# Copies of every second half issued by ScalarE in a graph attention kernel

## The chip, the cores and the metric

The kernel runs on one core of a Trainium2 chip. The metric is the device time of one execution in microseconds (us), from three runs of the kernel before. One further execution was profiled; the rows below are its.

## The reference

A pre-normed graph attention layer over 12,500 nodes with 128 features and 200,000 edges, sorted by target node, with 64 features each. There are four heads of 32 features.

```python
h = jnp.maximum(_layernorm(x), 0.0)
h = (h @ W_node.T).reshape(num_nodes, H, HD)
e = (edge_features @ W_edge.T).reshape(num_edges, H, HD)
att = jnp.sum(jnp.concatenate([h[src], h[tgt], e], axis=-1) * a, axis=-1)
att = jnp.where(att > 0, att, 0.2 * att)
m = jnp.maximum(segment_max(att, tgt), 0.0)
ex = jnp.exp(att - m[tgt])
denom = segment_sum(ex, tgt) + (num_edges - deg)[:, None] * jnp.exp(-m)
h_prime = segment_sum((ex / denom[tgt])[:, :, None] * h[src], tgt)
x = x + h_prime.reshape(num_nodes, H * HD)
```

## The kernel before

**Front.** The nodes are taken in 14 groups of 7 blocks of 128. VectorE computes mean and variance; VectorE, ScalarE and Pool normalise 2, 1 and 4 of the 7 blocks (`ON_DVE`, `ON_ACT`, lines 257, 314, 377, 518); TensorE transposes and projects them (`project`, line 637); ScalarE copies the result out of PSUM in three pieces (`evacuate`, line 530), and SyncE stores it in a table in DRAM: per node 128 projected features and 4 source scores. `s_thirds` counts the first two pieces, for the last group only. TensorE's next projection waits until all three pieces of the group before are out (`rows`).

**Edges.** Edges lie in 1563 tiles of 128, and a tile that touches two blocks of target nodes takes two slots: 1660 slots are in use, in 52 groups of 32, each of two halves of 16. One group is one turn of the loop, fully unrolled, in which each engine has its own program, called `body` (lines 866 to 1382); engines meet only in semaphores:

- Pool gathers the table rows of one tile at a time with an indirect DMA into a ring of 32 tiles (`gather`, line 156; loop at line 899). Eight at a time, it first waits until the ring's old tiles have been copied out (`copied`).
- SyncE copies slots from the ring into one of three half-group buffers, `halves` (`copies`, line 815). Eight copies make a batch. For each batch it loads four gather counts and eight ring places from SBUF into registers (lines 825 and 829), waits until all earlier copies have landed (line 833) and until the gathers have (line 835), and then issues eight DMAs of 66 KB. Half `h` must wait for `vals` of half `h - 3`, whose buffer it takes (line 817). In turn `g` SyncE loads flags (842), the edge features (846), stores edge scores (850, which waits for ScalarE's `edge_out`), and then issues the copies of halves `2g + 3` and `2g + 4`.
- VectorE (`body`, line 1350) adds up the scores: `zs` at line 1191 waits for all 32 copies of its group. Then come running maxima per target, the argument of the exponential (1266), the weighted rows of each half (`weighted_rows`, 1274, whose end is the semaphore `vals`), a one-hot matrix of targets per half (`make_onehot`, 1162), and the addition of TensorE's sums to the accumulator (`adds`, 1323).
- TensorE (`body`, line 997) forms the sums as one-hot times rows, three slots at a time in six batches a half (`sums`, 960), the target scores (`target_parts`, 950), the edge scores of a later group (937) and the targets per slot (`slot_targets`, 915). The last waits for `edge_out` of the tile group five ahead. In turn `g` three batches of the first half stand behind it.
- ScalarE (`body`, line 1101) takes two exponentials and a rescaling factor (1061, 1065, 1071), starts the load of the keys (1050), copies the edge scores out of PSUM (`edge_scores_out`, 1023, the semaphore `edge_out`), turns the keys into a one-hot matrix in two passes (`compare_keys`, 1053) and casts the targets (`targets_out`, 1029). In the last turn, 51, it also makes the two one-hots (`last_onehot`, 1122), from absolute difference and rectifier, and in turn 50 it issues the last four copies (`last_copies`, 1135).

The order on each engine is the order of the calls in its `body`. A finishing stage normalises and adds `x`.

Of the kernel before, what the change touches and what calls it, by code (L numbers as in the profile page):

```python
# [14 lines left out]
P = 128  # L15
# [4 lines left out]
G = 32  # L20
# [29 lines left out]
def gat_kernel(nc, x, src, tiles, tile_ends, ea, w_node, w_edge, a, out):  # L50
# [12 lines left out]
    with ctx:  # L63
# [97 lines left out]
        with ExitStack() as stage:  # L161
# [95 lines left out]
            ON_DVE, ON_ACT = 2, 1  # L257
# [4 lines left out]
            with nc.Block(no_gpsimd_drain=True) as block_:  # L262
                @block_.sync
                def _(sp):
# [5 lines left out]
                    def store_last(g):  # L270
                        for n, (b0, b1) in enumerate(((0, 3), (3, 6), (6, W))):
                            if n < 2:
                                sp.wait_ge(s_thirds, n + 1)
                            else:
                                sp.wait_ge(n_["rows"], g + 1)
# [33 lines left out]
                def _(pool):  # L309
                    def normalise(g):  # L310
# [3 lines left out]
                        for w in range(ON_DVE + ON_ACT, W):  # L314
# [26 lines left out]
                def _(dve):  # L341
# [31 lines left out]
                    def normalise(g):  # L373
# [3 lines left out]
                        for w in range(ON_DVE if g else W):  # L377
# [129 lines left out]
                def _(act):  # L507
# [6 lines left out]
                    def normalise(g):  # L514
# [3 lines left out]
                        for w in range(ON_DVE, ON_DVE + ON_ACT):  # L518
# [11 lines left out]
                    def evacuate(g):  # L530
# [5 lines left out]
                        first = S.copy(rows[:, q, 0:3, :], v3(h_bank[0], WP))  # L536
                        second = S.copy(rows[:, q, 3:6, :], v3(h_bank[1], WP))
                        S.copy(rows[:, q, 6, :], h_bank[2]).then_inc(n_["rows"], 1)
                        if g + 1 == N_NODE_GROUPS:
                            first.then_inc(s_thirds, 1)  # L540
                            second.then_inc(s_thirds, 1)
# [81 lines left out]
                def _(pe):  # L623
# [13 lines left out]
                    def project(g):  # L637
                        pe.wait_ge(n_["hn_t"], g + 1)
                        if g:
                            pe.wait_ge(n_["rows"], g)  # L640
                        else:
                            pe.wait_ge(s_wp, 1)
                        for n in range(W):
                            last = T.matmul(h_bank[n // 3][:, (n % 3) * WP:(n % 3 + 1) * WP], hn_t[g % 2][:, n * P:(n + 1) * P], w_proj[:, :],
# [109 lines left out]
        with ExitStack() as stage:  # L754
# [57 lines left out]
            with nc.Block() as block:  # L812
                @block.sync
                def _(sp):
# [51 lines left out]
                    def body(g, prev, nxt, second):  # L866
# [9 lines left out]
                        for h in (2 * g.n + 3, 2 * g.n + 4):  # L876
                            if h < 2 * NG:
                                copies(h, range(GS // BATCH if h < 2 * NG - 1 else 1))

# [31 lines left out]
                def _(pe):  # L911
# [48 lines left out]
                    def sums(g, a, batches):  # L960
# [10 lines left out]
                        if 0 in batches:  # L971
                            pe.wait_ge(s["vals"], g.n * 2 + a + 1)
                            pe.wait_ge(s["onehot"], g.n * 2 + a + 1)
# [46 lines left out]
                def _(act):  # L1020
# [37 lines left out]

                    def exponentials(g):
# [62 lines left out]
                    def last_onehot(g, a, count):  # L1122
                        of_slot = sel_f[:, 0, 0:GS + LAST]
# [402 lines left out]
```

## Time and profile before

| what | value |
|---|---|
| median of 3 runs | 2974.41 us (2969.7 to 2981.4) |
| profiled execution, its own time | 3012.78 us |
| its span | 3011.0 us, granted TensorE clock 0.649 |
| busy: PE, VectorE, ScalarE, Pool | 1245.5, 1442.5, 558.8, 1529.1 us |
| gathers by Pool | 1563, mean 949 ns |
| copies from the ring by SyncE | 1656 of 66 KB; four more by ScalarE |

The span reaches from the first to the last instruction. The busy time leaves out the issuing of DMAs, so SyncE, which does nothing else, has no line there; its work is seen in the timeline of its queue (SPq). "Idle before" in a row is the engine's idle time just ahead, with what ended it.

### The profile page before, as it was taken

How to read it: one execution, taken by the hardware profiler on the slowest of the kernel's cores; microseconds unless marked ns; L12 is line 12 of the kernel's file. 1: busy time of each engine (PE TensorE's matmuls, PEld its weight loads, DVE VectorE, ACT ScalarE, POOL GpSimd, SP SyncE). 2: the span in 40 equal slices, each digit the busy share in tenths (PEclk: the TensorE clock that was granted, in tenths of full speed). 3: DMA queues.
4: the chain of work that ended last, by engine and by line, in shares of the span. 5: the costliest groups of instructions: out<-in, count | busy, mean ns of one | idle time of the engine just before them, and what ended most of it. 6: DMA issues, size and time to landing. Idle time of an engine off the chain costs nothing. (4 is left out here: it accounts for less than half of the span.)

```text
span 3011.0 us, 30562 instructions
## 1 busy us (share of the span) xinstructions
PE 1245.5 (41%) x7204; PEld 932.6 (31%) x7205; DVE 1442.5 (48%) x3419; ACT 558.8 (19%) x629; POOL 1529.1 (51%) x1634
## 2 busy tenths in 40 slices
PE   5432534434434434434353343444344434333335
PEld 5222423323322323323232232333233223223333
DVE  8334545345344445445364453544444534544448
ACT  6211212112111211112111121121121211211213
POOL 6654545555554555555455555555455545554540
PEclk9766656666656666667666666666666656655667
DMA  6443434444344434444343344444344443333335
GB/s 228 147 136 100 136 111 122 118 110 123 114 110 117 119 108 129 115 114 135 107 124 119 108 136 111 116 124 115 109 123 109 136 117 96 112 95 95 95 88 165
DMA packets 333239, 360.72 MB, mean 120 GB/s; under 512 B 57725, under 2 KB 289565, under 8 KB 320135
## 3 DMA queue, kind: packets, MB, share of 16 engines
q1 hardware_dynamic: 272231, 191.42, 20.5%
q0 software_dynamic: 50304, 107.57, 15.7%
q10 hardware_dynamic: 10528, 59.78, 6.1%
q8 instruction: 62, 1.02, 0.1%
q14 instruction: 114, 0.93, 0.1%
HBM read 229.63 MB, written 18.57 MB: 82 GB/s over the span
## 5 line engine op out<-in xcount | busy, mean ns | idle before, releaser
L157 POOL DMA_INDIRECT gath<-node_table,src_i x1563 | 1483.5, 949 | 1385.7 <-DMA gath<-gath 875.6
L979 PE MATMUL bank<-vals,onehot 128*128 128x137 f32 x1992 | 438.5, 389 | 231.0 <-issue 159.6
L979 PEld LDWEIGHTS bank<-vals,onehot 128*128 128x128 f32 x1992 | 412.3, 290 | 259.1 <-issue 192.7
L979 PE MATMUL ps_oht<-vals,onehot 128*128 128x137 f32 x1328 | 304.2, 393 | 191.1 <-issue 160.8
L1334 DVE TENSOR_TENSOR acc<-acc,bank 128x411 f32 x374 | 198.0, 529 | 381.5 <-remote 232.7
L1191 DVE TENSOR_TENSOR zs<-gath,te 128x128 f32<-128x128 f32 x52 | 19.7, 379 | 741.4 <-DMA gath<-gath 561.2
L979 PEld LDWEIGHTS ps_oht<-vals,onehot 128*128 128x128 f32 x1328 | 281.6, 293 | 210.5 <-issue 182.7
L970 PE MATMUL bank<-block_1h,zero_b 128*128 128x411 bf16 x311 | 117.7, 430 | 491.5 <-issue 263.1
L1061 ACT ACTIVATE bank<-arg 128x128 f32<-128x128 f32 x52 | 14.6, 281 | 1515.8 <-DVE arg L1266 1410.5
L1334 DVE TENSOR_TENSOR acc<-acc,ps_oht 128x411 f32 (+1 forms) x248 | 131.6, 531 | 262.2 <-remote 167.1
L956 PE MATMUL bank<-tgt_slot,onehot_t 128*128 128x12 bf16 x1664 | 84.9, 182 | 373.8 <-issue 361.7
L1278 DVE TENSOR_TENSOR vals<-gath,bank 128x2048 f32<-128x2048 f32 x104 | 236.8, 2277 | 0.0
L1166 DVE TENSOR_TENSOR onehot<-bank,rel_s 128x2048 f32<-128x2048 f32 x102 | 232.6, 2281 | 0.0
L970 PE MATMUL ps_oht<-block_1h,zero_b 128*128 128x411 bf16 x208 | 81.1, 429 | 338.7 <-issue 186.3
L1055 ACT ACTIVATE onehot_t<-onehot_t,pcol 128x4096 bf16<-128x4096 bf16 x50 | 185.3, 3707 | 97.7 <-DMA onehot_t<-key_rows 75.5
L970 PEld LDWEIGHTS bank<-block_1h,zero_b 128*128 128x128 bf16 x311 | 28.8, 105 | 556.0 <-issue 299.8
L956 PEld LDWEIGHTS bank<-tgt_slot,onehot_t 128*128 128x128 bf16 x1664 | 68.9, 100 | 383.8 <-issue 369.3
L1057 ACT ACTIVATE onehot_t<-onehot_t,iota 128x4096 bf16<-128x4096 bf16 x50 | 185.4, 3708 | 1.6
L937 PE MATMUL bank<-eattr,w_eatt 128*32 128x512 f32 x360 | 181.8, 651 | 1.7 <-issue 1.7
L970 PEld LDWEIGHTS ps_oht<-block_1h,zero_b 128*128 128x128 bf16 x208 | 19.7, 104 | 384.8 <-issue 212.3
L1031 ACT CAST tgt_slot<-bank 128x384 bf16<-128x384 f32 x52 | 24.7, 476 | 389.5 <-remote 384.2
L1027 ACT COPY edge_out<-bank 32x512 f32<-32x512 f32 x49 | 28.2, 575 | 282.6 <-PE bank L937 183.6
(240 smaller groups left out, 1256.8 us busy)
## 6 DMA issues: line engine op xcount, KB each, us to landing
gath<-gath SPq DMA_DIRECT2D x1656, 66.0 KB
onehot_t<-key_rows ACTq DMA_DIRECT2D x52, 1024.0 KB
eattr<-edge_attr_in SPq DMA_DIRECT2D x43, 1024.0 KB
gath<-node_table,src_i POOLq DMA_INDIRECT x1563
node_table<-onehot SPq DMA_DIRECT2D x13, 462.0 KB, 3.5
acc<-x_in SPq DMA_DIRECT2D x10, 448.0 KB, 5.5
edge_s<-edge_scores SPq DMA_DIRECT2D x11, 256.0 KB
edge_scores<-edge_out SPq DMA_DIRECT2D x43, 64.0 KB
```

The source lines that it names most:

```text
L157: nc.gpsimd.indirect_dma_start(out=ring[:, t % RING, :], out_offset=None, in_=table, in_offset=bass.IndirectOffsetOnAxis(ap=src_i[:, t:t + ...
L937: last = T.matmul(ps_edge, w_eatt[:, c, :], eattr_of(t)[:, c, :], start=(c == 0), stop=(c == 3))
L956: last = T.matmul(ps_te[:, 3 * HEADS * slot:3 * HEADS * (slot + 1)], onehot_t[:, slot, :], tgt_slot[:, :, slot], start=True, stop=True)
L970: T.matmul(SUM_BANK[n % DEPTH][:, 0:SPAN * ACC], zero_b[:, :], block_1h[:, 0:SPAN * ACC], start=True, stop=False)
L979: last = T.matmul(at, onehot[:, a, j, :], vals[:, a, j, :], start=not wide, stop=j == BATCHES[b][-1])
L1027: S.copy(edge_out[:, t % 2, :], ps_edge).then_inc(s["edge_out"], 1)
L1031: S.copy(tgt_slot[:, :, :].rearrange("p c s -> p (c s)"), ps_tgt_slot).then_inc(s["tgt_slot"], 1)
L1055: S.activation(onehot_t[:, :, :], onehot_t[:, :, :], ACT.Abs, bias=pcol[:, 0:1], scale=-1.0).then_inc(s["apart"], 1)
L1057: S.activation(onehot_t[:, :, :], onehot_t[:, :, :], ACT.Relu, bias=iota[:, 1:2], scale=-1.0).then_inc(s["oht"], 1)
L1166: V.tensor_tensor(onehot[:, a, :, :], ps_iota.unsqueeze(1).broadcast_to((P, GS, P)), rel_s[:, ds(g.n * G + a * GS, GS)].unsqueeze(2).broad ...
L1278: V.tensor_tensor(vh[:, :, :, 0:HD], halves[:, (2 * g.n + a) % 3, 0:count, 0:NODE_DIM].rearrange("p s (h c) -> p s h c", h=HEADS), ex.unsq ...
L1334: V.tensor_tensor(a_blk, a_blk, SUM_BANK[(done_batches(g, a, b) - 1) % DEPTH][:, 0:wide * ACC], ALU.add).then_inc(s["added"], 1)
```

## The change

In the front, `ON_DVE` becomes a list: 2 for groups 0 to 11, then 3 and 4, so Pool does 3 and 2 blocks in the last two groups. Every group's first two pieces are counted by `s_thirds`, and `project` waits for the piece of PSUM that it overwrites rather than for all three.

In the loop, ScalarE issues the copies of half `2g + 3` in turns 0 to 49, after the load of keys and ahead of `edge_scores_out`, `compare_keys` and `targets_out`. The new function is like SyncE's. It waits for `vals` first and loads its registers then. SyncE keeps half `2g + 4`, and the eight copies of the last half that it had. The conditions between copies are the same: each batch still waits until all earlier ones have landed.

In turn 50 too ScalarE makes the two one-hots in place of VectorE; they and those of turn 51 count in `last_apart` alone, and TensorE waits for that.

```diff
-            ON_DVE, ON_ACT = 2, 1
+            ON_DVE, ON_ACT = [2] * (N_NODE_GROUPS - 2) + [3, 4], 1
...
                     def project(g):
                         pe.wait_ge(n_["hn_t"], g + 1)
-                        if g:
-                            pe.wait_ge(n_["rows"], g)
-                        else:
+                        if not g:
                             pe.wait_ge(s_wp, 1)
                         for n in range(W):
+                            if g and n == 6:
+                                pe.wait_ge(n_["rows"], g)
+                            elif g and n % 3 == 0:
+                                pe.wait_ge(s_thirds, 2 * g - 1 + n // 3)
...
                             store_edges(t)
-                        for h in (2 * g.n + 3, 2 * g.n + 4):
-                            if h < 2 * NG:
-                                copies(h, range(GS // BATCH if h < 2 * NG - 1 else 1))
-
+                        if second:
+                            copies(2 * g.n + 4)
+                        if g.n + 2 == NG:
+                            copies(2 * NG - 1, range(1))
...
                             pe.wait_ge(s["vals"], g.n * 2 + a + 1)
-                            pe.wait_ge(s["onehot"], g.n * 2 + a + 1)
+                            if g.n + 2 < NG:
+                                pe.wait_ge(s["onehot"], g.n * 2 + a + 1)
+                            else:
+                                pe.wait_ge(s["last_apart"], 2 * (2 * (g.n + 2 - NG) + a + 1))
...
+                    def copies(h):
+                        act.wait_ge(s["vals"], h - 2)
+                        for b in range(GS // BATCH):
+                            n = h * (GS // BATCH) + b
+                            if n == 3 * (GS // BATCH):
+                                act.wait_ge(s_landed, 4)
+                            _, ready = nc.values_load_multi_w_load_instructions(
+                                ready_row[:, n * READY:(n + 1) * READY], engines=[mybir.EngineType.Activation], min_val=16 * BLK, max_val=16 * BLK * -(-NB_TILES // READY))
+                            _, places = nc.values_load_multi_w_load_instructions(
+                                place_row[:, n * BATCH:(n + 1) * BATCH], engines=[mybir.EngineType.Activation], min_val=0, max_val=RING - 1,
+                                skip_runtime_bounds_check_because="the front masks the places with the ring's length less one")
+                            act.wait_ge(s["copied"], 16 * BATCH * n)
+                            for q, landed in enumerate(ready):
+                                act.wait_ge(s_g[q], landed)
+                            for j, place in enumerate(places):
+                                act.dma_start(halves[:, h % 3, b * BATCH + j, :], ring[:, ds(place, 1), :].rearrange("p o r -> p (o r)")).then_inc(s["copied"], 16)
...
-                        if not nxt:
+                        if not second:
                             last_onehot(g, 0, GS)
                         exponentials(g)
                         rescale_factor(g)
-                        if not nxt:
-                            last_onehot(g, 1, LAST)
                         if g.n + 2 == NG:
                             last_copies(g + 1)
+                        if not second:
+                            last_onehot(g, 1, GS if nxt else LAST)
                         if (g.n + 2) % CG == 0 and (g.n + 2) // CG < NCH:
                             cast_sel((g.n + 2) // CG)
                         if second:
                             load_keys(g + 2)
+                            copies(2 * g.n + 3)
                         if g.n + AHEAD < NTG:
                             edge_scores_out(g.n + AHEAD)
...
                         weighted_rows(g, 0)
-                        if nxt:
+                        if second:
                             make_onehot(g, 0)
...
                         weighted_rows(g, 1, GS if nxt else LAST)
+                        if second:
+                            make_onehot(g, 1)
                         if nxt:
-                            make_onehot(g, 1)
                             key_flags(g + 1)
```

Two places show how instructions move. The first is ScalarE's program in one turn, from its load of the keys to its next exponential. Before:

```order
L1050 DMA onehot_t<-key_rows 128x4096 [waits scores_ps]
L1027 COPY edge_out<-bank 32x512 [waits edge_scores_stored0,edge_ps]
L1055 ACTIVATE onehot_t<-onehot_t,pcol 128x4096 [waits key_rows_loaded]
L1057 ACTIVATE onehot_t<-onehot_t,iota 128x4096 [waits apart]
L1031 CAST tgt_slot<-bank 128x384 [waits tgt_slot_ps]
L1061 ACTIVATE bank<-arg 128x128 [waits arg]
```

Of the change the same turn, the end of the second batch of copies first, up to the start of the next turn's copies:

```order
L1076 DMA gath<-gath 128x132
L1029 COPY edge_out<-bank 32x512 [waits edge_scores_stored0,edge_ps]
L1057 ACTIVATE onehot_t<-onehot_t,pcol 128x4096 [waits key_rows_loaded]
L1059 ACTIVATE onehot_t<-onehot_t,iota 128x4096 [waits apart]
L1033 CAST tgt_slot<-bank 128x384 [waits tgt_slot_ps]
L1080 ACTIVATE bank<-arg 128x128 [waits arg]
L1084 ACTIVATE enm<-m 128x128 [waits vals,m]
L1090 ACTIVATE alpha<-cols,first_ind 128x4 [waits scaled,cols]
L1052 DMA onehot_t<-key_rows 128x4096 [waits scores_ps]
L1067 TENSOR_LOAD rows_i [waits vals]
L1067 ISA x8
L1069 TENSOR_LOAD rows_i
```

Between the load of the keys and the copy of edge scores there now stand two batches, each two register loads with eight instructions on registers and eight copies, behind waits for `vals`, gathers and landings. ScalarE's program grows from 619 rows to 2525.

The second place is SyncE's program, from the last copy of a half on (`ISA` is an instruction on registers). Before, ahead of the second of the two halves of a turn:

```order
L837 DMA gath<-gath 128x132
L825 TENSOR_LOAD rows_i [waits vals]
L825 ISA x8
L829 TENSOR_LOAD rows_i
L837 ISA [waits tiles_gathered2,tiles_gathered1,tiles_gathered3,tiles_gathered0,copied]
```

Of the change:

```order
L836 DMA gath<-gath 128x132
L841 DMA flag_row<-chunk_flags 4x2x128 [waits cfirst]
L845 DMA eattr<-edge_attr_in 128x2048 [waits edge_ps]
L849 DMA edge_scores<-edge_out 32x4x128 [waits edge_out]
L824 TENSOR_LOAD rows_i [waits vals]
L824 ISA x8
L828 TENSOR_LOAD rows_i
L836 ISA [waits tiles_gathered2,tiles_gathered1,tiles_gathered3,tiles_gathered0,copied]
```

After one half SyncE goes straight to the next turn's loads and to the store that waits for `edge_out`. TensorE's order in the loop is unchanged.

## Rows read from the trace of the kernel before

**Rows 1.** The page: busy time of each engine.

```profile
PE 1245.5 (41%) x7204; PEld 932.6 (31%) x7205; DVE 1442.5 (48%) x3419; ACT 558.8 (19%) x629; POOL 1529.1 (51%) x1634
```

**Rows 2.** Waits: who waited for whom, us in total, times, longest.

```profile
DVE zs L1191 <- DMA gath<-gath: 561.2, 37, 28.4
...
SPq L835 <- DMA gath<-node_table,src_i: 32.9, 42, 1.4
```

**Rows 3.** Source line 1191: durations in ns, first and last start in us.

```profile
L1191 DVE TENSOR_TENSOR zs<-gath,te x52: 376/379/382, 166.8 to 2952.1; 128x128 f32<-128x128 f32 x52
```

**Rows 4.** Timeline of SyncE, 1669 to 1722 us: start, us, what, count.

```profile
1669.77 13.69 SPq L837 DMA_DIRECT2D gath<-gath  x8
...
1669.77 23.39 SPq L837 DMA_DIRECT2D gath<-gath  x16
...
1695.98 0.73 SPq L850 DMA_DIRECT2D edge_scores<-edge_out  x1
1708.75 12.36 SPq L837 DMA_DIRECT2D gath<-gath  x16
```

**Rows 5.** Timeline of VectorE in the same group.

```profile
1665.62 0.38 DVE L1191 TENSOR_TENSOR zs<-gath,te 128x128 f32<-128x128 f32 x1 [13.29 <-DMA gath<-gath]
...
1666.92 1.73 DVE L1334 TENSOR_TENSOR acc<-acc,bank 128x411 f32 x3
...
1688.35 0.26 DVE L1282 TENSOR_TENSOR vals<-enm,last_s 128x64 f32<-128x64 f32 x1
...
1723.17 0.38 DVE L1191 TENSOR_TENSOR zs<-gath,te 128x128 f32<-128x128 f32 x1 [13.11 <-issue]
```

**Rows 6.** Timeline of SyncE at 1538 us, eight copies.

```profile
1538.21 5.04 SPq L837 DMA_DIRECT2D gath<-gath  x8
```

**Rows 7.** Timeline of Pool: its gathers, 1661 to 1706 us.

```profile
1661.11 0.94 POOL L157 DMA_INDIRECT gath<-node_table,src_i  x1 [1.89 <-issue]
...
1678.81 0.94 POOL L157 DMA_INDIRECT gath<-node_table,src_i  x1 [0.30 <-issue]
...
1704.94 0.94 POOL L157 DMA_INDIRECT gath<-node_table,src_i  x1 [0.30 <-issue]
```

**Rows 8.** Timeline of PE, matmuls, 1671 to 1709 us.

```profile
1671.97 0.84 PE L956 MATMUL bank<-tgt_slot,onehot_t 128*128 128x12 bf16 x24
...
1683.73 2.87 PE L979 MATMUL bank<-vals,onehot 128*128 128x137 f32 x12
...
1698.99 1.74 PE L979 MATMUL bank<-vals,onehot 128*128 128x137 f32 x6 [5.04 <-issue]
...
1708.08 0.39 PE L979 MATMUL ps_oht<-vals,onehot 128*128 128x137 f32 x1 [1.71 <-issue]
```

**Rows 9.** Timeline of ScalarE, 1683 to 1698 us.

```profile
1683.96 0.28 ACT L1061 ACTIVATE bank<-arg 128x128 f32<-128x128 f32 x1 [27.32 <-DVE arg L1266]
1684.17 0.29 ACT L1065 ACTIVATE enm<-m 128x128 f32<-128x128 f32 x1
...
1690.42 0.57 ACT L1027 COPY edge_out<-bank 32x512 f32<-32x512 f32 x1 [5.76 <-issue]
...
1694.63 3.71 ACT L1057 ACTIVATE onehot_t<-onehot_t,iota 128x4096 bf16<-128x4096 bf16 x1
```

**Rows 10.** Timeline of ScalarE's queue: its four copies near the end.

```profile
2942.46 2.95 ACTq L1148 DMA_DIRECT2D gath<-gath  x4
```

**Rows 11.** Timelines of Pool and ScalarE at 2831 us.

```profile
2830.84 0.94 POOL L157 DMA_INDIRECT gath<-node_table,src_i  x1 [0.30 <-issue]
...
2831.53 0.28 ACT L1061 ACTIVATE bank<-arg 128x128 f32<-128x128 f32 x1 [33.42 <-DVE arg L1266]
2832.93 0.31 ACT L1065 ACTIVATE enm<-m 128x128 f32<-128x128 f32 x1 [1.12 <-remote]
```

**Rows 12.** The one-hots: VectorE's group, and ScalarE's sixteen pieces in turn 51.

```profile
L1166 DVE TENSOR_TENSOR onehot<-bank,rel_s 128x2048 f32<-128x2048 f32 x102 | 232.6, 2281 | 0.0
...
2953.90 4.78 ACT L1130 ACTIVATE onehot<-iota,sel_f 128x128 f32<-128x128 f32 x16 [8.24 <-PE bank L979]
```

More of the change, by code:

```diff
@@ L272, in store_last @@
                             if n < 2:
-                                sp.wait_ge(s_thirds, n + 1)
+                                sp.wait_ge(s_thirds, 2 * g + n + 1)
                             else:
@@ L313, in normalise @@
                             pool.wait_ge(n_["hn_t_ps"], g - 1)
-                        for w in range(ON_DVE + ON_ACT, W):
+                        for w in range(ON_DVE[g] + ON_ACT, W):
                             last = pool.tensor_scalar(hn[g % 2][:, w, :], xg[g][:, w, :], mv[:, g % DEEP, w, 0:1], rstd[:, g % DEEP, w:w + 1],
@@ L376, in normalise @@
                             dve.wait_ge(n_["hn_t_ps"], g - 1)
-                        for w in range(ON_DVE if g else W):
+                        for w in range(ON_DVE[g] if g else W):
                             last = V.scalar_tensor_tensor(out=hn[g % 2][:, w, :], in0=xg[g][:, w, :], scalar=mv[:, g % DEEP, w, 0:1],
@@ L517, in normalise @@
                             act.wait_ge(n_["hn_t_ps"], g - 1)
-                        for w in range(ON_DVE, ON_DVE + ON_ACT):
+                        for w in range(ON_DVE[g], ON_DVE[g] + ON_ACT):
                             last = S.activation(hn[g % 2][:, w, :], xg[g][:, w, :], ACT.Relu, bias=shift[:, g % DEEP, w:w + 1],
@@ L535, in evacuate @@
                             act.wait_ge(n_["tgt"], g - 1)
-                        first = S.copy(rows[:, q, 0:3, :], v3(h_bank[0], WP))
-                        second = S.copy(rows[:, q, 3:6, :], v3(h_bank[1], WP))
+                        S.copy(rows[:, q, 0:3, :], v3(h_bank[0], WP)).then_inc(s_thirds, 1)
+                        S.copy(rows[:, q, 3:6, :], v3(h_bank[1], WP)).then_inc(s_thirds, 1)
                         S.copy(rows[:, q, 6, :], h_bank[2]).then_inc(n_["rows"], 1)
-                        if g + 1 == N_NODE_GROUPS:
-                            first.then_inc(s_thirds, 1)
-                            second.then_inc(s_thirds, 1)
                     def weights():
@@ L1122, in last_onehot @@
                     def last_onehot(g, a, count):
-                        of_slot = sel_f[:, 0, 0:GS + LAST]
-                        if a == 0:
+                        first, done = (g.n + 2 - NG) * G + a * GS, 2 * (2 * (g.n + 2 - NG) + a)
+                        of_slot = sel_f[:, 0, 0:G + GS + LAST]
+                        if done == 0:
                             act.wait_ge(s["edge_turned"], NCH)
-                            S.copy(of_slot, rel_s[:, ds(g.n * G, GS + LAST)]).then_inc(s["last_rel"], 1)
+                            S.copy(of_slot, rel_s[:, ds(g.n * G, G + GS + LAST)]).then_inc(s["last_rel"], 1)
                             act.wait_ge(s["last_rel"], 1)
@@ L1129, in last_onehot @@
                         for j in range(count):
-                            last = S.activation(onehot[:, a, j, :], iota[:, 0:P], ACT.Abs, bias=of_slot[:, a * GS + j:a * GS + j + 1], scale=-1.0)
+                            last = S.activation(onehot[:, a, j, :], iota[:, 0:P], ACT.Abs, bias=of_slot[:, first + j:first + j + 1], scale=-1.0)
                         last.then_inc(s["last_apart"], 1)
-                        act.wait_ge(s["last_apart"], a + 1)
-                        S.activation(onehot[:, a, 0:count, :], onehot[:, a, 0:count, :], ACT.Relu, bias=iota[:, 1:2], scale=-1.0).then_inc(s["onehot"], 1)
+                        act.wait_ge(s["last_apart"], done + 1)
+                        S.activation(onehot[:, a, 0:count, :], onehot[:, a, 0:count, :], ACT.Relu, bias=iota[:, 1:2], scale=-1.0).then_inc(s["last_apart"], 1)
                     def last_copies(g):
```

## Prediction

> **What bounds it now.** The busy times come first [rows 1]: no engine is busy for more than 51% of the span, so a chain of waits sets the time. The waits say which [rows 2]. VectorE starts a group with `zs`, which waits for the group's 32 copies from the ring (561 us in 37 waits with a named releaser). SyncE issues these copies, and it waits for almost nothing itself: 33 us for the gathers. So SyncE's own issuing is the bound. `zs` starts 52 times between 166.8 and 2952.1 us [rows 3]: 54.6 us a group.
>
> I take one group apart, from the `zs` at 1665.62 to the next at 1723.17, 57.5 us [rows 4, 5]. SyncE spends it so:
> - a: 1665.62 to 1669.77, register loads before the next half, 4.2 us;
> - b: sixteen copies of a first half, 23.4 us, eight of them taking 13.7;
> - c: 1693.16 to 1708.75, three loads and stores and another register load, 15.6 us;
> - d: sixteen copies of a second half, 12.4 us, and 2.1 us from the end of the last issue to `zs`.
>
> The sum is 57.7, of which 0.1 is rounding: SyncE has no slack at all. Eight copies take 5.04 us elsewhere [rows 6], so the same instructions can cost 2.7 times as much. The expensive stretches lie under Pool's gathers: one run of gathers goes from 1661.11 to 1679.75, and the next ends at 1705.88 [rows 7], and the copies become slow some 6 us after a run begins and quick again 2 to 3 us after it ends. PE shows the same: the fourteen matmul records from 1698.99 on need until 1708.47 there, the last with 1.71 us of idle time before it [rows 8]. I call this a gather stretch, without claiming its cause. A register load costs 12.36 − 2 × 5.04 = 2.3 us outside one, and 1708.75 − 1696.71 = 12.0 us inside.
>
> VectorE is not the bound: its first-half rows are finished at 1688.61 [rows 5], 20 us before SyncE reaches the half that needs them.
>
> **The change, part by part, for this group.**
>
> *Piece c leaves the chain.* ScalarE issues the second half. It may begin once the first half has landed (1693.16 + 2.1 = 1695.3), once `vals` is there (1688.61) and once it has loaded its registers, which by the code it does only after `vals`. Were all that free, 1708.75 becomes 1695.3: a gain of 13.5 us.
>
> *PE becomes later.* `slot_targets` waits for `edge_out`, and the three batches of sums behind it on PE's queue wait with it. ScalarE made that copy at 1690.42 [rows 9]; now it stands behind sixteen copies, so it comes about when the next group starts. The queued work is fourteen matmul records: 14 × 2.87 / 12 = 3.3 us at the pace of 1683.73, but 9.5 us from 1698.99 to 1708.47 [rows 8]. VectorE adds these sums 1.3 us after `zs` [rows 5], so `vals` comes later by 2.0 us at best and 8.2 at worst. I take 5, the middle, because half of the group lies in gather stretches. `vals` is then at 1693.6.
>
> *ScalarE's register load.* No row shows one in this loop's stretches. The ends are SyncE's 2.3 and 12.0. ScalarE's own four late copies took 2.95 us [rows 10], 0.74 each, near SyncE's quick 0.63, but no gather ran then. In a gather stretch ScalarE isn't spared: with gathers running at 2831 its two exponentials start 1.40 us apart, at 1684 only 0.21 [rows 9, 11]. I take the middle, 7.2: the second half starts at 1693.6 + 7.2 = 1700.8. The gain shrinks to 8.0 us.
>
> *Piece a.* SyncE's store of edge scores waits for `edge_out`, and its register load stands behind that store. The copy on ScalarE ends 0.6 us after its last issue, 1.5 us before `zs`; with 0.7 for the store and 7.2 for the load the first half starts 6.4 us after `zs` rather than 4.2. That loses 2.2. Its ends are a gain of 2.7 and a loss of 7.0.
>
> *ScalarE's copies.* Quick, they cost what SyncE's do; with eight in a gather stretch 13.7 − 5.0 = 8.7 more. I take a third, 3: the load before them often uses the stretch up.
>
> Net: 8.0 − 2.2 − 3.0 = 2.8 us a group. ScalarE gets fifty halves, so 140 us.
>
> *Compare and targets on ScalarE.* `compare_keys`, two passes of 3.71 us [rows 9], and the cast of the targets now run after the copies, and end some 6 us after `zs`. PE wants them there: `target_parts` started at 1671.97, 6.3 us after `zs` [rows 8]. I cost them at nothing; the cover is those 6 us of PE's first three batches, and without it each late microsecond goes on to `vals`.
>
> *Last groups.* VectorE loses two one-hots of 2.28 us; ScalarE gets twice sixteen pieces of 0.30 and a pass over each half [rows 12], where it idles for over 20 us. Ends 0 and 4.6; I take 2. *Node groups:* Pool loses three rows of 128 columns, VectorE gets three, about 0.3 us each by the like-sized pieces of rows 12; counting by thirds lets PE start each projection before ScalarE's last copies end. What hides this is that the loop's first `zs` stands at 166.8 us [rows 3], behind gathers and key rows: 1 us, ends −1 and 3.
>
> Sum against the profiled execution: 3012.8 − 140 − 3 = 2870. The median of the runs is 2974.4, 38.4 lower, so 2832 for the median, 4.8% faster.
>
> Here a rule speaks against the change. The rows show SyncE issuing for the whole group and ScalarE idle for 27 us before its exponential [rows 9]. The Trainium skill, "DMA: Bandwidth & Descriptors", section "Issuing engines are not separate DMA queues", says that DMAs from different engines run on the same DMA engines, and that spreading them saves only the sequencer's issue time, usually small. By that rule the sum would be the small terms alone, about 2971; by the rows the sequencer's time is what is short.
>
> **Rivals.**
> 1. *ScalarE is slowed as SyncE is, and the detour over it closes a longer chain* (slower). New chain: `zs`, PE's six batches, `vals`, ScalarE's register load and copies, `zs`. For it: rows 8 and 11. Against it: an engine that has idled may start quickly. With PE 8.2 late and the load at 12.0, the second half starts at 1708.8, no gain; with the 2.2 of piece a each group loses 2.2: +110 us, 3081. It decides as soon as lateness of `vals`, load and slower copies together take more than the 13.5 us.
> 2. *A larger gain*: ScalarE, fresh, is not slowed and PE's lateness stays under the 4.4 us by which `vals` has slack with a quick load (1695.3 − 1688.61 − 2.3). Pool's 30 gathers at 1.25 us apart (1563 in 52 groups, [rows 7]) would then fill 37.6 of some 50 us, and with them two thirds of another slow batch (8.7) comes back: 13.5 − 5.8 = 7.7 us a group, 385 us in all, 2586.
> 3. *No change*: the `copied` waits keep batches strictly one after another, so two queues never copy at once; the saved 13.5 goes into `vals` waits and slower batches. 2971.
>
> **How the numbers follow.** Forecast 0.46, rival 1 0.24, rival 2 0.22, rival 3 0.08. The forecast's own range is 2740 to 2930 (net 4.6 to 0.8 us a group). The whole range, 2580 to 3070, reaches to rival 2 and nearly to rival 1's price; wider ends would need every register load in the same kind of stretch. 0.5%, 15 us, is about what a measurement of this kernel tells from no change. Faster by more: forecast and rival 2, 0.68; within: 0.08; slower: 0.24.
>
> **What would show it.** Right: the distance between `zs` near 52 us; second halves on ScalarE's queue starting 5 to 8 us after the first half's last issue; `vals` some 28 us after `zs` instead of 23. Wrong: ScalarE's exponential or PE's `target_parts` waiting for ScalarE's copies; `vals` over 31 us after `zs` (rival 1); ScalarE's sixteen copies taking over 20 us; or a distance under 50 us (rival 2). SyncE should then show real waits, on `edge_out` and on landings, which it doesn't have now.

## The result, and the profile after

The changed kernel takes 3134.0 us (median of 6 runs, 3100.2 to 3156.1); the kernel before takes 2981.2 us (6 runs). The ratio is 1.0449, with a 95% interval of 1.0405 to 1.0493: 4.5% slower, where 4.8% faster was forecast, and outside the range of 2580 to 3070. That ratio leaves out slow executions, two of the changed kernel's six among them (3148.2 and 3156.1 us), so it is smaller than that of the two medians, 1.051. The profiled execution is the one of 3148.2 us, and its span is 3146.4 us; the same kernel profiled again at 3125.8 us (e12, below) shows the same waits.

The waits of the changed kernel come first (engine, line, what it waited for: us in total, times, longest):

```profile
DVE acc L1355 <- remote: 1100.7, 87, 19.8
ACT edge_out L1029 <- DMA gath<-gath: 1071.1, 35, 36.9
...
DVE zs L1212 <- DMA gath<-gath: 286.0, 46, 18.9
```

and in e12:

```profile
DVE acc L1355 <- remote: 1060.2, 89, 19.9
```

`zs` no longer waits long for copies: 286 us, against 561 in [rows 2]. But VectorE now waits 1101 us before its additions of PE's sums (`acc`, line 1355), 87 times, up to 19.8 us. "Remote" means that the wait ended with a semaphore of another engine beside which no instruction stands. This row was in the trace of the kernel before too, and I did not read it. Nor did I read ScalarE's row, for its cast of PE's `slot_targets`:

```profile
DVE acc L1334 <- remote: 399.8, 61, 10.9
ACT tgt_slot L1031 <- remote: 384.2, 41, 17.9
```

So the change took 275 us out of one wait and put 701 us into another. One group shows how. VectorE, from the `zs` at 811.28 to the next at 875.44, 64.2 us (start, length, engine, line; in brackets the idle time before it):

```profile
811.28 0.38 DVE L1212 TENSOR_TENSOR zs<-gath,te 128x128 f32<-128x128 f32 x1 [5.07 <-DMA gath<-gath]
...
827.33 1.31 DVE L1355 TENSOR_TENSOR acc<-acc,ps_oht 128x411 f32 x2 [14.65 <-remote]
...
855.47 0.58 DVE L1355 TENSOR_TENSOR acc<-acc,ps_oht 128x411 f32 x1 [16.77 <-remote]
855.97 2.28 DVE L1299 TENSOR_TENSOR vals<-gath,bank 128x2048 f32<-128x2048 f32 x1
...
858.30 0.26 DVE L1303 TENSOR_TENSOR vals<-enm,last_s 128x64 f32<-128x64 f32 x1
```

PE in the same group, its records of sums (line 981) and what surrounds them:

```profile
811.58 2.87 PE L981 MATMUL ps_oht<-vals,onehot 128*128 128x137 f32 x12
814.29 0.40 PE L981 MATMUL bank<-vals,onehot 128*128 128x137 f32 x2
...
833.77 1.10 PE L981 MATMUL bank<-vals,onehot 128*128 128x137 f32 x8
834.80 3.62 PE L936 MATMUL bank<-eattr,w_eatt 128*32 128x512 f32 x8
```

And Pool's gathers:

```profile
804.08 0.95 POOL L157 DMA_INDIRECT gath<-node_table,src_i  x1 [16.61 <-DMA gath<-gath]
...
822.84 0.95 POOL L157 DMA_INDIRECT gath<-node_table,src_i  x1 [0.31 <-issue]
832.30 0.95 POOL L157 DMA_INDIRECT gath<-node_table,src_i  x1 [8.51 <-DMA gath<-gath]
...
851.07 0.94 POOL L157 DMA_INDIRECT gath<-node_table,src_i  x1 [0.30 <-issue]
```

PE's records end at 814.7, and VectorE adds these sums at 827.33, 12.6 us later. The next ones are recorded by 834.9, and the first of them is added at 855.47, 20.6 us later. The trace also holds the times of the semaphore's updates: they stand at 827.13 to 827.25 and at 855.27 to 855.39, so VectorE starts as soon as the semaphore comes, and it is the semaphore that is late. Both additions come 3.5 us after a run of gathers ends (823.79 and 852.01).

VectorE made the same first addition 1.3 us after `zs` in the kernel before [rows 5]. PE's sums weren't outside a run there either: the ones behind `slot_targets` stand at 1698.99 to 1708.47 [rows 8], under a run that ends at 1705.88, and their semaphores are recorded by 1709.04. But VectorE adds them only after the next `zs`, at 1723.17:

```profile
1724.47 0.56 DVE L1334 TENSOR_TENSOR acc<-acc,bank 128x411 f32 x1
```

So their lateness had 14 us of room. Now PE starts the sums with `zs`, since `slot_targets` ahead of them on its queue waits for the `edge_out` that ScalarE copies in the same turn, and the run has then been going since 804.08. There is no room left.

ScalarE and SyncE show the rest of the chain (ACTq and SPq are their DMA issues):

```profile
838.07 0.28 ACT L1080 ACTIVATE bank<-arg 128x128 f32<-128x128 f32 x1 [10.05 <-issue]
...
861.02 12.99 ACTq L1076 DMA_DIRECT2D gath<-gath  x16
874.11 0.58 ACT L1029 COPY edge_out<-bank 32x512 f32<-32x512 f32 x1 [35.34 <-DMA gath<-gath]
```

```profile
821.16 17.19 SPq L836 DMA_DIRECT2D gath<-gath  x16
...
874.71 0.31 SPq L849 DMA_DIRECT2D edge_scores<-edge_out  x1
```

`vals` ends at 858.56, 47.3 us after `zs`, where it took 23.0 [rows 5]. ScalarE's copies follow at once and are quick: 2.5 us for the register load, 12.99 for all sixteen. SyncE has finished its half at 838.35, and its store of the edge scores comes only at 874.71, once `edge_out` is there.

The changed kernel holds its own counter-example. In turns 4, 20 and 41 the run of gathers under way at `zs` was a short one of eight. Turn 20, VectorE, Pool and ScalarE:

```profile
1358.88 0.38 DVE L1212 TENSOR_TENSOR zs<-gath,te 128x128 f32<-128x128 f32 x1 [4.77 <-DMA gath<-gath]
...
1363.36 0.58 DVE L1355 TENSOR_TENSOR acc<-acc,bank 128x411 f32 x1 [3.08 <-PE ps_oht L981]
...
1398.01 0.38 DVE L1212 TENSOR_TENSOR zs<-gath,te 128x128 f32<-128x128 f32 x1 [7.84 <-DMA gath<-gath]
```

```profile
1360.47 0.95 POOL L157 DMA_INDIRECT gath<-node_table,src_i  x1 [0.30 <-issue]
```

```profile
1396.54 0.57 ACT L1029 COPY edge_out<-bank 32x512 f32<-32x512 f32 x1 [21.69 <-DMA gath<-gath]
```

The run ends at 1361.42, 2.5 us after `zs`; the first addition follows 4.5 us after `zs`, as soon as PE has formed the sums; and the group takes 39.1 us (38.0 and 38.4 in turns 4 and 41), where the kernel before took 47.6 to 49.9 in these turns. (The turn after each takes 68 us: there a longer run is under way at `zs`, and the first addition comes 20.5 to 21.2 us after it.) `edge_out` stands behind sixteen copies here as in every other turn. So neither ScalarE's copies nor the late `edge_out` are slow by themselves; they are where the sums meet a run.

A second one stands at the end. The last edge scores are copied at the end of turn 42, which still holds up the sums behind it (turn 43 takes 65.3 us). From turn 44 on nothing holds them. The starts of `zs` at turns 3, 43, 44 and 50, after:

```profile
327.97 0.38 DVE L1212 TENSOR_TENSOR zs<-gath,te 128x128 f32<-128x128 f32 x1 [5.05 <-DMA gath<-gath]
...
2685.35 0.38 DVE L1212 TENSOR_TENSOR zs<-gath,te 128x128 f32<-128x128 f32 x1 [4.71 <-DMA gath<-gath]
...
2750.65 0.38 DVE L1212 TENSOR_TENSOR zs<-gath,te 128x128 f32<-128x128 f32 x1 [5.71 <-DMA gath<-gath]
...
3055.68 0.38 DVE L1212 TENSOR_TENSOR zs<-gath,te 128x128 f32<-128x128 f32 x1 [6.86 <-issue]
```

and before:

```profile
336.33 0.38 DVE L1191 TENSOR_TENSOR zs<-gath,te 128x128 f32<-128x128 f32 x1 [12.74 <-DMA gath<-gath]
...
2539.55 0.38 DVE L1191 TENSOR_TENSOR zs<-gath,te 128x128 f32<-128x128 f32 x1 [13.83 <-issue]
...
2597.90 0.38 DVE L1191 TENSOR_TENSOR zs<-gath,te 128x128 f32<-128x128 f32 x1 [13.76 <-issue]
...
2919.61 0.38 DVE L1191 TENSOR_TENSOR zs<-gath,te 128x128 f32<-128x128 f32 x1 [9.52 <-DMA gath<-gath]
```

From turn 3 to 43 a group takes 2357.4 / 40 = 58.9 us after and 55.1 before; from 44 to 50 it takes 305.0 / 6 = 50.8 after and 53.6 before. In these six groups the change gains 2.8 us a group. Groups scatter between 40 and 61 us, but other traces agree: 50.8 in e12, and 48.6 in e3 against 52.8 in e4 on the same chip. That it is the forecast's own 2.8 is chance, since the forecast had lateness of PE and of SyncE's store in it, which these groups don't have.

### The profile page after: what moved, and what is told of

Same layout as the page of the kernel before. It is cut to its first block and busy times, and to the rows that moved or that the text cites. A ratio compares the mean times of both kernels' runs of the same rounds, so it can differ in the third digit from the quotient of the medians.

```text
span 3146.4 us, 30596 instructions
## 1 busy us (share of the span) xinstructions
PE 1280.9 (41%) x7205; PEld 918.7 (29%) x7205; DVE 1432.2 (46%) x3420; ACT 565.3 (18%) x663; POOL 1529.9 (49%) x1631
## 5 line engine op out<-in xcount | busy, mean ns | idle before, releaser
L981 PE MATMUL bank<-vals,onehot 128*128 128x137 f32 x1992 | 428.6, 382 | 175.2 <-DVE onehot L1187 87.8
L981 PEld LDWEIGHTS bank<-vals,onehot 128*128 128x128 f32 x1992 | 405.2, 284 | 197.3 <-issue 180.2
L936 PE MATMUL bank<-eattr,w_eatt 128*32 128x512 f32 x360 | 243.5, 776 | 119.4 <-issue 118.7
L923 PE MATMUL bank<-block_1h,tgt_t 98*128 98x32 bf16 x624 | 25.1, 187 | 502.2 <-issue 502.2
L923 PEld LDWEIGHTS bank<-block_1h,tgt_t 98*128 98x128 bf16 x624 | 21.8, 104 | 515.3 <-issue 514.9
L936 PEld LDWEIGHTS bank<-eattr,w_eatt 128*32 128x32 f32 x360 | 41.6, 122 | 290.7 <-issue 287.7
```

The costliest lines, as they stand in the source:

```text
L923: last = T.matmul(ps_tgt_slot[:, c * G:(c + 1) * G], tgt_t[0:N_BLOCKS, c, :], block_1h[0:N_BLOCKS, ds(g.n * G, G)], start=True, stop=True)
L936: last = T.matmul(ps_edge, w_eatt[:, c, :], eattr_of(t)[:, c, :], start=(c == 0), stop=(c == 3))
L981: last = T.matmul(at, onehot[:, a, j, :], vals[:, a, j, :], start=not wide, stop=j == BATCHES[b][-1])
```

## The experiments

Theory A: PE's sums, held by `slot_targets` until `zs`, fall into the run of gathers just when VectorE needs them, and their semaphores reach it only when the run ends. Theory B: the chain over ScalarE (`vals`, register load, sixteen copies) is too long wherever `edge_out` stands.

**e1.** ScalarE's `body`:

```diff
+                        if g.n + AHEAD < NTG:
+                            edge_scores_out(g.n + AHEAD)
                         if second:
                             copies(2 * g.n + 3)
-                        if g.n + AHEAD < NTG:
-                            edge_scores_out(g.n + AHEAD)
```

> The changed kernel with one move: ScalarE copies the edge scores (edge_out) ahead of its sixteen ring copies, not behind them. Theory A (PE's slot_targets waits for edge_out, so the sums behind it run when a run of gathers is already going, and their semaphores reach VectorE only when that run ends): VectorE's first add comes back from 16 us after zs to 1.3 us, vals of the first half from 45 us to about 22 to 28, and the groups look like the changed kernel's own groups 44 to 49, which have no edge scores left to copy: 50.8 us each, so about 2830 to 2860 us in all. Theory B (the chain over ScalarE is too long by its register loads and copies, wherever edge_out stands): the groups stay at 57 us or more, over 3050 us.

**e2.** TensorE's `body`:

```diff
                         sums(g, 0, range(3))
+                        sums(g, 0, range(3, NB))
                         if second:
                             slot_targets(g + 2)
-                        sums(g, 0, range(3, NB))
```

> The changed kernel with PE's slot_targets moved behind all six sums of its group; ScalarE's order stays as changed. Theory A: the sums no longer wait for edge_out, so the first add is back at 1.3 us after zs, as in e1; slot_targets itself is as late as in the changed kernel. About 2830 to 2900 us. Theory B (the sums are not what counts, but the late targets, compare_keys and target_parts): no gain, 3080 to 3150 us.

**e3.** The kernel before with `copies` on ScalarE and SyncE issuing `2 * g.n + 4` alone:

```diff
-                        for h in (2 * g.n + 3, 2 * g.n + 4):
-                            if h < 2 * NG:
-                                copies(h, range(GS // BATCH if h < 2 * NG - 1 else 1))
+                        if second:
+                            copies(2 * g.n + 4)
+                        if g.n + 2 == NG:
+                            copies(2 * NG - 1, range(1))
...
```

> The kernel before with ScalarE's copies alone; one-hots, thirds and the split of the node groups as before. Theory A and theory B both put the whole loss here: within 0.5% of the changed kernel, 3120 to 3150 us. Were the one-hots of group 50 or the node groups to blame, it would be near 2975.

**e4.** The changed kernel with the same lines the other way round, and no `copies` on ScalarE.

> The changed kernel with all copies back on SyncE: one-hots of group 50 on ScalarE, thirds and the split of the node groups stay. Theory A and B: the prediction's small terms alone, 2 + 1 us, so 2965 to 2980 us; if these parts cost anything, over 2990.

Measured, all against the same kernel before (2982.0 us):

| | median us | ratio, 95% interval |
|---|---|---|
| e1 edge scores first | 2957.9 | 0.989 (0.984 to 0.995) |
| e2 sums first | 2938.4 | 0.986 (0.979 to 0.993) |
| e3 copies alone | 3124.2 | 1.041 (1.031 to 1.050) |
| e4 all but the copies | 2980.1 | 0.9985 (0.995 to 1.002) |

e3 and e4 put the whole loss on ScalarE's copies; one-hots, thirds and node groups are worth nothing that can be measured. e1 and e2 take the loss away by order alone, without touching copies or registers: theory A. VectorE's "remote" waits go with it. The rows of e3, e4, e1 and e2, in this order:

```profile
DVE acc L1352 <- remote: 1054.1, 86, 19.8
```

```profile
DVE acc L1354 <- remote: 398.8, 56, 13.3
```

```profile
DVE acc L1355 <- remote: 428.9, 52, 28.6
```

```profile
DVE acc L1355 <- remote: 558.9, 52, 20.5
```

In e2's turn 19 the first addition is back at 1.3 us:

```profile
1207.19 0.38 DVE L1212 TENSOR_TENSOR zs<-gath,te 128x128 f32<-128x128 f32 x1 [13.79 <-DMA gath<-gath]
...
1208.50 0.56 DVE L1355 TENSOR_TENSOR acc<-acc,ps_oht 128x411 f32 x1
```

The times asked for were missed, though. For e1 2830 to 2860 us was expected and for e2 2830 to 2900, and against the kernel before they are only 1.1 and 1.4% faster, less than the 2% that counts as faster here. The first additions are early, but later ones of the same group still fall into a run: in this turn of e2 the fourth comes 24.0 us after `zs`.

**e5 to e7.** The stretch itself was then tried. After every gather Pool writes some unused columns:

```diff
                             gather(t)
+                            if paced:
+                                pool.wait_ge(s_idle, paced)
+                            for w in range(4):
+                                pool.memset(pool_idle[:, 8 * w:8 * w + 8], 0.0).then_inc(s_idle, 1)
+                            paced += 4
```

e5 is this in the kernel before, e6 the same with one memset for four, e7 this in e2.

> The kernel before with four small memsets on Pool (8 columns each, on one partition) after every gather, to space the gathers out by about 0.5 us, from 1.25 to some 1.7 us; 30 gathers a group then take about 51 us. Theory C (the slowing of SyncE and of PE's semaphores comes from gathers issued faster than something can follow, since it sets in only some 6 us into a run): SyncE's copies stay at 0.65 us each and the group falls to what Pool allows, some 51 us or less, 2700 to 2850 us. Theory D (any gather under way slows the others, whatever the distance): slow stretches cover nearly the whole group, and the time rises over 3050 us.

> The kernel before with one memset after every gather, spacing some 0.1 to 0.2 us longer. Theory C: slow stretches begin later in a run and shrink, 2850 to 2960 us. Theory D: a little slower than before, 2980 to 3050 us.

> e2 (PE's sums ahead of slot_targets, 2938 us) with the four memsets of e5. Theory C: two issuing queues and no slow stretches; Pool is then the bound, near 51 us a group, 2700 to 2800 us. Theory D: over 3000 us.

Against a kernel before of 2978.8 us: e5 2690.2, ratio 0.903 (0.901 to 0.906); e6 2997.7, 1.007 (1.003 to 1.011); e7 2630.3, 0.883 (0.880 to 0.886). More work on Pool makes the kernel 10% faster. Theory D (any gather under way slows the others) falls. But theory C's number (gathers spaced 1.7 us apart) doesn't hold either: in e5 they are 1.31 us apart, and what also differs is that Pool pauses now and then, waiting for its own semaphore:

```profile
1204.56 0.95 POOL L157 DMA_INDIRECT gath<-node_table,src_i  x1 [0.15 <-issue]
1205.51 0.20 POOL L915 MEMSET pool_idle<- 1x8 f32 x4
1205.87 0.95 POOL L157 DMA_INDIRECT gath<-node_table,src_i  x1 [0.15 <-issue]
1207.70 0.21 POOL L915 MEMSET pool_idle<- 1x8 f32 x4 [0.88 <-remote]
1208.06 0.95 POOL L157 DMA_INDIRECT gath<-node_table,src_i  x1 [0.15 <-issue]
```

**e8 to e11.** e8 is e5 with twelve memsets of two columns. e9 has one memset and waits for it before the next gather:

```diff
                             gather(t)
+                            pool.memset(pool_idle[:, 0:8], 0.0).then_inc(s_idle, 1)
+                            paced += 1
+                            pool.wait_ge(s_idle, paced)
```

e10 is the changed kernel with e5's memsets, e11 has them with the orders of e1 and e2 together.

> The kernel before with twelve memsets of two columns after every gather, where e5 had four; four brought the distance of gathers in a run from 1.25 to only 1.31 us, plus pauses of 1 to 2 us after 6 to 10 gathers. Twelve add 8 x 0.037 us: a distance of 1.6 us. Theory C1 (what counts is the distance, every bit of it helps): no pauses and no slow stretch, SyncE's eight copies at 5.0 us throughout, Pool's 30 gathers then fill 48 us, the group is near 48 to 50 us, 2650 to 2750 us. Theory C2 (what counts in e5 is that Pool pauses, since it waits for its own semaphore, which comes late as PE's do): still pauses, time near e5's 2690 or worse by the longer distance, 2690 to 2800 us.

> The kernel before with one memset after every gather as in e6, but now Pool waits for that memset's own semaphore before the next gather. Theory C2: the wait closes the loop at every gather, so pauses come back and the time falls clearly below e6's 2998 us, to 2700 to 2850 us. Theory C1: one memset and its wait bring the distance to about 1.3 to 1.4 us by themselves; a gain without pauses, if any.

> The changed kernel as it is with the four memsets of e5. Theory A (the loss lies in sums that fall into a slow stretch): without slow stretches the late edge_out costs only the few us that ScalarE's copies take, so the change loses its 4.5% and comes near e7 (2630 us), 2640 to 2700 us, no slower than e5 (2690 us). Theory B (a chain over ScalarE that is too long anyway): slower than e5 by 3% or more, over 2770 us.

> e7 (slot_targets behind the sums, four memsets) with ScalarE's copy of the edge scores ahead of its ring copies too, the candidate for the best version. If the late edge_out still costs something in e7 (its vals come 27 us after zs, 23.9 in e5), it is faster than 2630 us, 2560 to 2620 us; if nothing of the two orders counts without slow stretches, 2630 us.

These four ran on another chip, on which the kernel before takes 2110.7 us: 29% less than on the others, with the same code. Measured there: e8 2673.3, e9 2336.0, e10 2285.3, e11 2284.8 us, all slower than the kernel before (ratios 1.267, 1.107, 1.083 and 1.083). The expectations of times were made for the other kind of chip and say nothing here, but the traces do. In e10 the additions have no "remote" wait at all, only short ones for PE itself, and Pool is busy for 81% of the span:

```profile
DVE zs L1220 <- DMA gath<-gath: 556.5, 52, 22.9
DVE acc L1363 <- PE bank L989: 72.5, 58, 6.6
DVE acc L1363 <- PE ps_oht L989: 50.2, 39, 6.5
```

```profile
PE 1097.3 (48%) x7205; PEld 843.0 (37%) x7205; DVE 1437.9 (63%) x3420; ACT 564.5 (25%) x663; POOL 1853.5 (81%) x7803
```

So these traces show no slow stretch (SyncE's eight copies take 6.9 us at most in e8 to e11, where the kernel before has up to 15.3), and Pool's gathers run on almost without a break. e10 and e11 differ only in the two orders, and in time by 0.5 us. That says less than it seems: Pool sets the pace of both, so it would also hide a few microseconds of another chain.

**e12 to e14.** The changed kernel, e10 and e11, each word for word, to have them where stretches are slow.

> The changed kernel word for word, once more. The last four runs fell on a chip on which the kernel before takes 2111 us, not 2980, and whose traces show no slow stretch under the gathers. If this chip is of that kind: theory A says the change costs nothing there, since Pool's 30 gathers of 1.25 us a group set the pace and the sums aren't late: within 1% of the kernel before, 2095 to 2135 us; theory B (a chain over ScalarE too long anyway): over 2200 us. If it is of the other kind: 1.045 times the kernel before, as in the first comparison.

> e10 word for word (the changed kernel with four memsets after each gather). On a chip with slow stretches: theory A 2640 to 2700 us (e5, the kernel before with the same memsets, took 2690 us beside a kernel before of 2979), theory B over 2770 us. On a chip without: 2285 us again, bound by Pool.

> e11 word for word (sums ahead of slot_targets, edge scores ahead of ScalarE's copies, four memsets). On a chip with slow stretches: 2560 to 2620 us if the late edge_out still costs in e7 (2630 us), else 2630 us. On a chip without: 2285 us again.

Here the kernel before took 3031.5 us. e12: 3137.1, ratio 1.032 (1.023 to 1.042). e13: 2765.8, 0.913 (0.905 to 0.921). e14: 2667.1, 0.884 (0.875 to 0.893). The change loses again, a little less than the first time, most of that because the kernel before is slower on this chip. With the memsets it stands at 0.913, where e5 stood at 0.903 on its own chip: theory B's 3% is not there in the ratio, and theory A's "no slower" is missed by about one. By the times expected neither is met: 2765.8 us lies above A's 2640 to 2700 and just under B's 2770, beside a kernel before that is 1.8% slower than e5's. e13 to e14, 3.6%, is what the two orders are worth while some stretches are still slow; where the traces show none it was nothing. e14's ratio is that of e7 (0.883), so the copy of the edge scores ahead of the ring copies adds nothing to the sums' order. The waits of e13 and of e14:

```profile
DVE acc L1363 <- remote: 712.8, 126, 18.5
```

```profile
DVE acc L1363 <- remote: 373.6, 68, 21.0
```

**e15 to e17.** e15 is e11 with e9's memset and wait in place of four memsets, e16 is e8 word for word, e17 is e11 without memsets.

> e14 (both orders) with one memset and a wait for that memset's own semaphore before the next gather, in place of four memsets. In e9, on the chip without slow stretches, this gave a distance of 1.32 us, as four memsets do. On a chip with slow stretches: theory C2 (Pool must be held by its own semaphore) says as good as e14 or better, 0.84 to 0.89 of the kernel before; theory C1 (only the distance counts) says the same as e14, 0.88. Both fall if it is over 0.93.

> e8 word for word (the kernel before, twelve memsets; distance 1.52 us; 2673 us and no slow stretch on the chip where the kernel before takes 2111). On a chip with slow stretches: theory C1 (distance) says they are gone at 1.52 us: 2673 us again, SyncE's eight copies at 5.0 to 5.3 us, runs of gathers without pauses. Theory C2: slow stretches and pauses stay, 2700 to 2900 us. On a chip without: 2673 us again.

> e1 and e2 together (edge scores ahead of ScalarE's copies, PE's sums ahead of slot_targets), no memset. On a chip with slow stretches: what holds the sums after either move alone is the gather run itself, so no more than e2's gain, 0.975 to 0.99 of the kernel before. On a chip without: within 1% of the kernel before, where both would be bound by Pool.

Against 3024.6 us: e15 2911.2, ratio 0.963 (0.959 to 0.967); e16 2763.8, 0.913 (0.910 to 0.916); e17 2928.3, 0.966 (0.962 to 0.971). e15 is no better than e17, so one memset and waiting for it gain nothing, and by what was expected both theories fall: C1 (only the distance counts) and C2 (Pool must be held by its own semaphore). C2 was hardly put to the test, though. Pool's waits for its memsets, in e14 and in e15:

```profile
POOL pool_idle L914 <- remote: 254.4, 181, 2.4
```

```profile
POOL gath L157 <- POOL pool_idle L911: 157.8, 510, 1.4
```

In e15 Pool was held for 0.3 us at a time on average, in e14 for 1.4 and up to 2.4. Whether such pauses are what helps was not tested. e17's 3.4% is more than the 1 to 2.5% expected of the two orders. e16 shows that at twelve memsets, 1.52 us apart, the slow stretches are gone on this kind of chip as well: SyncE's eight copies take 6.3 us at most. The additions hardly wait:

```profile
DVE acc L1342 <- remote: 40.5, 25, 2.9
```

but Pool's gathers and memsets fill most of the time, and it takes 3% more than e8's 2673 us, where C1 said the same. Nor does the distance explain e15: its gathers are 1.32 us apart and e14's 1.31, and e14 is 8% faster by its ratio.

**e18.** e11 with eight memsets of four columns.

> Both orders and eight memsets a gather, distance 1.31 + 4 x 0.026 = 1.42 us (four memsets gave 1.31, twelve 1.52). On a chip with slow stretches: twelve memsets left no slow copy at all (0 of 207 batches over 7 us) but Pool bound the group at 50.5 us; four left 57 of 207. If eight are enough, the group falls to Pool's bound, 48.8 x 1.42 / 1.52 = 45.6 us, or 46 to 48 us with the pauses, 0.84 to 0.86 of the kernel before. If the threshold lies above 1.42 us: as e14, 0.88. On a chip without: Pool's bound, about 2500 us.

It fell on a chip without slow stretches: 2447.9 us against 2109.0, ratio 1.161 (1.158 to 1.163). So at how many memsets between four and twelve the stretches end stays open.

## Why the prediction was wrong

The step that failed is *PE becomes later*. It priced the wait of the sums behind `edge_out` at 5 us, from 2.0 to 8.2, by how long PE's records take in a stretch [rows 8]. That is the wrong row: in the group shown fourteen records take 3.1 us, no longer than in quiet time. What is late is the semaphore by which VectorE learns of them. First additions moved from 1.3 to 16.0 us after `zs`, later ones by another 16.8, and `vals` by 24.3 us instead of 5. Two rows of the kernel before carry this price: VectorE's 399.8 us of "remote" waits before `acc`, up to 10.9 us each, and ScalarE's 384.2 us before the cast of the targets, up to 17.9. One of the latter stands in the very group that the prediction takes apart:

```profile
1693.14 0.46 PE L924 MATMUL bank<-block_1h,tgt_t 98*128 98x32 bf16 x12
```

```profile
1708.96 0.48 ACT L1031 CAST tgt_slot<-bank 128x384 bf16<-128x384 f32 x1 [10.62 <-remote]
```

PE's records of `slot_targets` end at 1693.60, and ScalarE casts them at 1708.96, 15.4 us later and 3.1 us after the run of gathers. With such a value as the upper end instead of 8.2, and two of them in a chain, rival 1 would have had the larger chance.

The other steps, in order:
- *What bounds it* was right: SyncE's issuing. With half of it moved, SyncE idles and `zs` waits 275 us less for copies.
- *Piece c leaves the chain*: right in direction. Its 13.5 us were never seen: turns 44 to 50, where neither the lateness behind `edge_out` nor the store of edge scores is in the way, gain 2.8 us. By the prediction's own terms some 10 us should be left there (an estimate: the 13.5 less 0.5 for the load and 3 for slower copies). Part of it went into later "remote" waits, 15 to 19 us in each of turns 47 and 48; how much is open.
- *ScalarE's register load*, 7.2 us (2.3 to 12.0): it takes 2.5. *ScalarE's copies*, 3 us more: sixteen take 12.99, so 0.6 more than SyncE's 12.36. In this group both lie in quiet time, because `vals` itself now comes only after a run has ended; of all of ScalarE's batches of eight copies, 8 of 100 take over 7 us.
- *Piece a*, a loss of 2.2 us: in the group shown, the first copy at 821.16 is 9.9 us after `zs`, against 4.2. The loss is 5.7, within its ends.
- *Last groups* and *node groups* at 3 us together: e4, 0.9985, can't be told from that or from nothing. *Compare and targets* at nothing: e4 doesn't have this term, since its copies are back on SyncE. In the group shown the cast ends at 818.24, 7.0 us after `zs`, and PE's `target_parts` starts only at 831.87, right behind the late sums, so it was covered there.
- The rule of the Trainium skill ("DMA: Bandwidth & Descriptors", section "Issuing engines are not separate DMA queues") would have given no change. No run shows that: the issue time saved was real (275 us less in `zs`'s wait), and e4 alone stands at no change. Nor does the rule speak of the wait that took the saving back.

Rival 1 had the sign, at 3081 us. Of the three parts in its sum two were real, lateness of `vals` (24.3 us where it had 8.2) and piece a (5.7 where it had 2.2); ScalarE's slow load (12.0) was not. The lateness alone was larger than all three together. The tests named in the prediction did tell: `vals` over 31 us after `zs`, and SyncE waiting for `edge_out`.

The mechanism is shown by e1, e2 and e3, by turns 4, 20 and 41, and by e13 against e14: the sums must fall into a slow stretch at the moment when they are needed. e10 against e11 fits it, but Pool sets the pace there. Why a run of gathers delays semaphores stays open. Whether the unpaced change is even or better on a chip without slow stretches was not measured, since e12 fell on the other kind.

## What to carry to other kernels

When a step is moved behind a long one on an in-order engine, look for everything that waits for it, and then for what else is going on at the new moment: here a wait for one small copy moved three batches of sums from a place where 14 us of lateness did no harm to one where none was left. Read the waits of every engine on the new chain, also where they cost nothing yet: their longest values here, 10.9 us on VectorE and 17.9 on ScalarE, tell more of the cost (up to 19.8) than the lengths of PE's records do. And where a kernel suffers from such a stretch, try to slow down what causes it: four idle writes after each gather took 10% off the kernel before, and 11.6% with both orders in the changed one (e14, 2667 us against 3031; e7, with the sums' order alone, is as good at 11.7%). Those two are the best measured where stretches are slow; e14's kernel is 8% slower than the kernel before where they are not (e11).

## What the hardware showed

- The same kernel before took 2979 to 3032 us on some chips and 2109 to 2111 us on others. In the traces taken on the second kind (e8 to e11, e18) the slow stretch under the gathers isn't there. The kernel before itself was not traced there, so that this is the whole difference is likely but not shown.
- Where it is there, the gathers' own data is not late: by the packets in the trace of the kernel before, the last one of a gather ends about 2.2 us after its issue (median), and no more than 2.4 for the last gather of each long run. What is late are SyncE's instructions, one after another [rows 4], and semaphores from PE, to VectorE by up to 20 us and to ScalarE by 15 us in the group shown, until some 3 to 3.5 us after the run of gathers ends.
- Making Pool do more between gathers shrinks it: one memset nothing (1.007), four a good part (0.903; SyncE's longest eight copies fall from 15.3 to 9.2 us), twelve all of it, at the price of a busier Pool (0.913). The distance of the gathers alone (1.31 us with four memsets, 1.32 in e15, which gains nothing) doesn't explain it. What resource is short stays open.
